# Two PSUM copies moved from VectorE to ScalarE, and the first x transposes moved to the last quantise round

## The chip, the cores and the metric

One Trainium2 chip, all 8 of its cores, one program for all with different data. A core has TensorE (PE, matrix products and transposes into PSUM), VectorE (DVE), ScalarE (ACT), GpSimd (POOL, which here only issues transfers) and SyncE (SP, which only issues transfers). The metric is the device time in microseconds of the slowest core. There is no traffic between cores.

## The reference, cut to what matters

```python
def layer(x):            # x: 2 x 8192 x 1024, float32
    q, k, v = x @ Wq.T + bq, x @ Wk.T + bk, x @ Wv.T + bv   # 16 heads of 64
    q = rope_headaxis(q) / 8;  k = rope_headaxis(k)          # angle by head index
    # sliding window: a query sees keys from 256 before it to 256 after it
    ctx = softmax(q k^T + window mask) v
    x = layernorm(x + ctx @ Wo.T + bo)
    xd, wd = mx_fp6(x), mx_fp6(W)      # blocks of 32 along a row, scale = max|.|/7.5,
    return layernorm(x + xd @ wd.T + bias)   # values rounded to an e2m3 grid
```

## The kernel before

Each core owns 2048 rows of x (16 tiles of 128) and gets two more tiles on each side, 20 in all. Products of float32 matrices are made as three bf16 products: every operand is split into a high part (an ACT activation that writes bf16, `*_hi`) and a low part (a DVE subtraction, `*_lo`). `split_evac` does this pair for a PSUM bank: ACT first, DVE behind it. All ordering between engines is worked out from a list of operations: each names the buffers it reads and writes, and each engine runs its own in the order of the list. An operation also waits for the earlier writer of its buffer on its own engine. `barrier()` makes the next operation of every engine wait for the last of all of them.

The program has four parts.

1. **Weights** (to 198 us). Wq, Wk and a piece of Wv are loaded, transposed, folded with the rope factors, and split.
2. **Quantise rounds** (198 to 351 us). The ffn weight has 8 row tiles, two per round `jp` = 0 to 3. A round is 28 steps, `qsteps`: two chains of 14 (one on the `qsc` tiles, one on `wfp`) laid alternately, so steps 0, 2, 4 ... are the one and 1, 3, 5 ... the other. Steps 8 and 9, 16 and 17, 22 and 23 run on ACT, all others on DVE. Between the steps, at the positions in `ins_at`, `vblocks` are put in: blocks of 4 transposes on PE into one PSUM bank and a `split_evac`. Rounds 0 to 2 have 4 `wv_block`s each (banks `pb[0]`, `pb[1]`); rounds 0 and 1 have two `x_pre_block`s more (banks `pb[2]`, `pb[3]`), which transpose the first two x tiles, `x_tm`, into `x_hi`, `x_lo`. With six blocks they sit behind steps 3, 7, 11, 15, 19, 23, with four behind 5, 11, 17, 23. Round 3 has none. After its steps each round transposes its two ffn tiles (4 blocks, banks `pb[2]`, `pb[3]`), splits them into three staging buffers `wfst`, and POOL writes them out with 8 transfers, each waiting for the one before. With three buffers the fourth split of a round waits for the first pair of transfers. The weight tiles of the rounds come through SP's queue (`wraw<-wf`); the two `x_tm` loads of round 0 stand in that queue behind the first three of them. A barrier ends this part.
3. **Attention** (351 to 1915 us). Ten passes `p` of two tiles. A pass makes k and v of its tiles on PE (`proj2`, evacuated by ACT), transposes v back in 4 blocks, alternately in banks `pb[0]` and `pb[1]`, and copies each bank into `v_tm` (line 877, DVE). Passes 2 to 9 then run 8 attention groups, numbered 0 to 7 here (two query tiles times four groups of 4 heads). After groups 1 and 3 come the load and transposes of the next x tiles, after group 5 the q projection (not in pass 9). A group (`att_group`) has 5 key tiles: PE makes scores, ACT the exponential into `probs`, DVE multiplies the first and the last with a triangle mask, PE multiplies with `v_tm` into `cbank`. At its end ACT takes the logarithm and the exponential of the row of sums (`zr`). The division follows one group later, in `tail`: PE spreads `zr` over 64 rows of `pb[3]`, DVE copies that to `zb_sb` and multiplies `cbank` with it into `ctxF`; `tail_split` then makes `cxh` and `cxl` on DVE. A tail is run after the last product of the next group and ahead of that group's `zr`. At most two pending pieces are run per group, so that behind a `spill` (after group 3) the pieces come in other pairs: groups 1 to 4 run tail and split together, group 5 spill and tail, groups 6 and 7 the split of the older group and then a tail. What is left is run at the start of the next pass (`flush_tail`).
4. **Output part** (from 1915 us): Wo, layernorms, quantised ffn. The change does not touch it.

Of the kernel before, what the change touches and what calls it, by code (L numbers as in the profile page):

```python
# [7 lines left out]
AF = mybir.ActivationFunctionType  # L8
# [176 lines left out]
def build_nc():  # L185
# [42 lines left out]
    pb = []  # L228
# [4 lines left out]
    pbuf = [Buf(f"pb{i}") for i in range(4)]  # L233
# [31 lines left out]
    def act(out_ap, in_ap, func, bias, scale, reads, writes, accum=None):  # L265
        P.op("act", lambda e, o=out_ap, i=in_ap, f=func, b=bias, s=scale,
             a=accum: e.activation(o, i, f, bias=b, scale=s, accum_out=a),  # L267
             reads=list(reads), writes=list(writes))
# [16 lines left out]
    def vcopy(eng, out_ap, in_ap, reads, writes):  # L285
        P.op(eng, lambda e, o=out_ap, i=in_ap: e.tensor_copy(o, i),  # L286
             reads=list(reads), writes=list(writes))
# [10 lines left out]
    def split_evac(psum_ap, psum_buf, hi_ap, lo_ap, wbufs):  # L298
        act(hi_ap, psum_ap, AF.Identity, 0.0, 1.0, [psum_buf], list(wbufs))
        tt("dve", lo_ap, psum_ap, hi_ap, ALU.subtract,  # L300
           [psum_buf] + list(wbufs), list(wbufs))
# [270 lines left out]
    x_tm_b = [Buf(f"x_tm{i}") for i in range(2)]  # L572
    x_fm_b = [Buf(f"x_fm{i}") for i in range(4)]

    def x_pre_block(j, half):
        fs = j
        bank = pb[2 + half]
        for k4 in range(4):
            kc = half * 4 + k4
            transp(x_tm[:, j * D + kc * 128: j * D + (kc + 1) * 128],  # L580
                   bank[:, k4 * 128:(k4 + 1) * 128], ident[:],
                   [x_tm_b[j], ident_b], [pbuf[2 + half]])
        split_evac(bank[:], pbuf[2 + half],
                   x_hi[:, fs * D + half * 512: fs * D + (half + 1) * 512],
                   x_lo[:, fs * D + half * 512: fs * D + (half + 1) * 512],
                   [x_fm_b[fs], wtmp_b[0], bias_tm_b["bq"]])
# [8 lines left out]
    for jp in range(4):  # L595
# [11 lines left out]
        vblocks = []  # L607
        if jp < 3:
            for vsl in range(2):
                vjt = 2 * jp + 2 + vsl  # L610
                for vhalf in range(2):
                    vblocks.append(
                        lambda vsl=vsl, vjt=vjt, vhalf=vhalf: wv_block(
                            wvraw[vsl][:], wvraw_b[vsl], vjt, vhalf, vhalf))
        if jp == 0:
            for j in range(2):
                dma_load("sp", x_tm[:, j * D:(j + 1) * D],
                         xp[j * 128:(j + 1) * 128, :],
                         [], [x_tm_b[j], (cosr_b, sinr_b)[j]])
        if jp < 2:  # L620
            for half in range(2):
                vblocks.append(
                    lambda j=jp, half=half: x_pre_block(j, half))
        ins_at = ((3, 7, 11, 15, 19, 23) if len(vblocks) > 4
                  else (5, 11, 17, 23))
        for i, f in enumerate(qsteps):
            f()
            if i in ins_at and ins_at.index(i) < len(vblocks):
                vblocks[ins_at.index(i)]()
        if jp < 2:  # L630
            for sl in range(2):
# [4 lines left out]
        for sl in range(2):  # L636
            jt = 2 * jp + sl
            st = jt % 3
            for half in range(2):
                bank = pb[2 + half]  # L640
                wi = (jt * 2 + half) % 3
                for k4 in range(4):
# [7 lines left out]
                                                    b=128),  # L650
                           wfst_lo[wi][:].rearrange("p (a b) -> p a b",
                                                    b=128),
                           [wfst_b[wi]])
                for scr, stg in ((wf_scr_hi, wfst_hi[wi]),
                                 (wf_scr_lo, wfst_lo[wi])):
                    dst = bass.AP(scr.tensor,
                                  scr.offset + (half * 4) * D + jt * 128,
                                  [[8 * D, 128], [D, 4], [1, 128]])
                    P.dma("gp", lambda e, d=dst, s=stg: e.dma_start(
                        out=d, in_=s[:].rearrange("p (a b) -> p a b",  # L660
                                                  b=128)),
# [16 lines left out]
    v_tm_b = [Buf(f"v_tm{i}") for i in range(VR)]  # L678
# [6 lines left out]
    zb_sb = sb("zb_sb", [64, 512], a_scope);  zb_sb_b = Buf("zb_sb")  # L685
# [48 lines left out]
    def att_group(tq, g):  # L734
# [18 lines left out]
        if True:  # L753
# [40 lines left out]
            def tail(g=g, cbank=cbank, cbank_b=cbank_b):  # L794
                mm(m4[0:1, 0:64], zr[:], pb[3][0:64, :], True, True,
                   [m4_b, zr_b], [pbuf[3]])
                vcopy("dve", zb_sb[:], pb[3][0:64, :], [pbuf[3]], [zb_sb_b])
                tt("dve", ctxF[:], cbank[0:64, :], zb_sb[:], ALU.mult,
                   [cbank_b, zb_sb_b], [ctxF_b])
            pending_tail.append(tail)  # L800

            def tail_split(g=g):
# [34 lines left out]
    for p in range(10):  # L837
        a = 2 * p
        j = a + 1
# [25 lines left out]
        for ti in range(2):  # L865
            vs = (a + ti) % VR
            for half in range(2):
                bank = pb[half]
                for c4 in range(4):
                    ch = half * 4 + c4  # L870
                    transp(q_fm[:, vscr_off + ti * D + ch * 128:
                                 vscr_off + ti * D + (ch + 1) * 128],
                           bank[:, c4 * 128:(c4 + 1) * 128], ident[:],
                           [vscr_bufs[ti], ident_b], [pbuf[half]])
                dst = strided(v_tm[:], vs * VW + half * 4 * 130,
                              [[130, 4], [65, 2], [1, 64]])
                vcopy("dve", dst,
                      bank[:].rearrange("p (a c b) -> p a c b", a=4, b=64),
                      [pbuf[half]], [v_tm_b[vs]])
        if 3 <= j <= 17:  # L880
            def projq(a=a, qsA=qsA, src_hi_fn=src_hi_fn,
                      src_lo_fn=src_lo_fn, src_bufs=src_bufs):
# [379 lines left out]
```

How the kernel before makes its waits and increments, by code:

```python
    def emit(self, eng_obj, eng_name, sems):  # L161
        for o in self.ops:
            if o.eng != eng_name:
                continue
            for k, v in o.waits:
                eng_obj.wait_ge(sems[k], v)
            if o.build is None:
                continue
            inst = o.build(eng_obj)
            if o.need_inc:
                inst.then_inc(sems[o.sem_key], 16 if o.is_dma else 1)
```

## Time and profile before

| | |
|---|---|
| median of the two runs | 2692.77 us (2626.21 and 2759.32) |
| the profiled execution | 2625.88 us; span of its slowest core 2624.3 us, of the eight 2611.6 to 2624.3 us |
| busy in the span | PE 1834.2 us (70%), DVE 800.1 (30%), ACT 670.1 (26%), POOL 58.2 (2%) |
| weights, 0 to 198 us | PE busy 41.5, DVE 89.2, ACT 40.2 |
| quantise rounds, 198 to 351 us | PE busy 28.9, DVE 93.7, ACT 44.0 |
| attention, 351 to 1915 us | PE busy 1322.7, DVE 292.8, ACT 416.6; mean granted PE clock 0.93 |
| output part, 1915 to 2624 us | PE busy 441.1, DVE 324.4, ACT 169.4; clock 0.78 |

How to read it: the busy shares are means over four parts with different limits. In the second part no engine is busy for much over half of the time, so what counts there is the order of dependent steps. In the third PE is busy for 85% of the time, and the question is what it waits for in the rest.

### The profile page before, as it was taken

Reading aid. Unit: us, or ns where it says so; the run is one execution under the profiler, and the core shown is the slowest. Engines: PE = TensorE matmul, PEld = TensorE weight load, DVE = VectorE, ACT = ScalarE, POOL = GpSimd, SP = SyncE. Lnnn points to the kernel's source line nnn. Section 1 sums busy time; section 2 is a strip of 40 time slices with the busy share of each in tenths; the row PEclk is TensorE's granted clock in tenths of the full one; section 3 lists DMA queues with packets and bytes.
Section 4 is the critical chain, followed back from the end, with each engine's and each line's share of the span. In section 5 each row is a group of like instructions: output and inputs, shape, how many; then the busy total and the mean of one; then the engine's idle time right before and its main releaser. Section 6 shows DMA issues by size and latency. Waiting matters only on the chain.

```text
span 2624.3 us, 36230 instructions; the slowest of 8 cores (2611.6 to 2624.3 us)
## 1 busy us (share of the span) xinstructions
PE 1834.2 (70%) x14760; PEld 1505.8 (57%) x14760; DVE 800.1 (30%) x1157; ACT 670.1 (26%) x1154; POOL 58.2 (2%) x92
## 2 busy tenths in 40 slices
PE   2212168978978878888789788788739767667444
PEld 2202157857757767667667567577528556556333
DVE  2467601021121121121221220211221455555443
ACT  1313311132232232222331322322312222222221
POOL 0001100000000000000000000000000000000000
PEclk9999999989989988999999989889859888888777
DMA  4103110000000000000000000000043011000000
GB/s 131 48 14 102 45 32 25 9 17 9 9 21 9 5 24 9 9 17 9 9 17 9 17 9 9 9 9 1 9 144 105 17 49 49 33 33 33 33 17 17
DMA packets 23711, 77.02 MB, mean 29 GB/s; under 512 B 3701, under 2 KB 4085, under 8 KB 23290
## 3 DMA queue, kind: packets, MB, share of 16 engines
q1 hardware_dynamic: 12250, 32.74, 4.1%
q0 software_dynamic: 7552, 25.17, 3.4%
q10 hardware_dynamic: 3744, 16.78, 2.1%
q8 instruction: 119, 1.95, 0.3%
q14 instruction: 46, 0.38, 0.0%
HBM read 53.71 MB, written 20.97 MB: 28 GB/s over the span
## 4 chain that ended last, share of the span: by engine, by line
PE 57%; DVE 21%; issue 9%; ACT 7%; DMA 5%; DVEq 1%; ACTq 0%; SPq 0%; POOL 0%; POOLq 0%
PE pb L257 42%; PE psE L258 5%; DVE probs L272 3%; PE pb L262 3%; PE psE L257 3%; ACT probs L267 3%; PE psO L258 2%; PE psO L257 2%; DVE x_hi L272 2%; ACT lnsc L267 1%; DVE qscW1b L272 1%; DVE ctxF L272 1%; DVE zb_sb L286 1%; DVE xdf_lo L272 1%; DVE xres L272 1%
## 5 line engine op out<-in xcount | busy, mean ns | idle before, releaser
L257 PE MATMUL pb<-probs,v_tm 128*65 128x128 f32 x2560 | 394.2, 303 | 193.3 <-DVE probs L272 193.3
L257 PEld LDWEIGHTS pb<-probs,v_tm 128*65 128x65 f32 x2560 | 312.3, 153 | 246.2 <-issue 229.7
L272 DVE TENSOR_TENSOR probs<-probs,m 128x512 f32<-128x512 f32 x128 | 88.2, 689 | 657.3 <-ACT probs L267 657.3
L267 ACT ACTIVATE probs<-psE,killb_sb 128x512 f32<-128x512 f32 x192 | 131.9, 687 | 288.9 <-PE psE L258 283.7
L257 PE MATMUL pb<-x_hi,wk_hi 128*128 128x256 bf16 x640 | 182.5, 285 | 24.8 <-DVE v_tm L693 23.1
L262 PE MATMUL pb<-ident,xdt 128*128 128x128 f32 x192 | 47.8, 409 | 200.3 <-DVE xdf_lo L272 103.4
L257 PE MATMUL pb<-x_lo,wk_hi 128*128 128x256 bf16 x640 | 182.6, 285 | 0.0
L257 PE MATMUL pb<-x_hi,wk_lo 128*128 128x256 bf16 x640 | 182.5, 285 | 0.0
L257 PE MATMUL pb<-x_hi,wv_lo 128*128 128x256 bf16 x640 | 174.4, 273 | 0.0
L257 PE MATMUL pb<-x_lo,wv_hi 128*128 128x256 bf16 x640 | 174.4, 273 | 0.0
L257 PE MATMUL pb<-x_hi,wv_hi 128*128 128x256 bf16 x640 | 174.4, 273 | 0.0
L286 DVE COPY v_tm<-pb 128x512 f32<-128x512 f32 x40 | 27.6, 691 | 463.0 <-PE pb L262 461.4
L258 PE MATMUL psE<-q_fm,k_fm 64*128 64x128 f32 x1536 | 157.7, 331 | 0.0
L262 PEld LDWEIGHTS pb<-ident,xdt 128*128 128x128 f32 x192 | 33.5, 210 | 213.9 <-issue 213.9
L258 PEld LDWEIGHTS psE<-q_fm,k_fm 64*128 64x128 f32 x1536 | 116.4, 213 | 55.1 <-issue 55.1
L257 PE MATMUL pb<-x_hi,wq_hi 128*128 128x256 bf16 x512 | 140.2, 274 | 0.0
L257 PE MATMUL pb<-x_hi,wq_lo 128*128 128x256 bf16 x512 | 140.1, 274 | 0.0
L257 PE MATMUL pb<-x_lo,wq_hi 128*128 128x256 bf16 x512 | 140.0, 273 | 0.0
L267 ACT ACTIVATE probs<-psO,killb_sb 128x512 f32<-128x512 f32 x128 | 87.7, 685 | 100.2 <-PE psO L258 100.2
L262 PE MATMUL pb<-ident,wraw 128*128 128x128 f32 x128 | 31.0, 423 | 105.9 <-DVE wraw L272 69.2
L267 ACT ACTIVATE k_fm<-pb,fm_bk 128x256 f32<-128x256 f32 x80 | 37.9, 474 | 230.6 <-PE pb L257 226.6
L272 DVE TENSOR_TENSOR xres<-pb,xres 128x512 f32<-128x512 f32 x32 | 22.1, 692 | 236.7 <-PE pb L262 232.9
(173 smaller groups left out, 3383.6 us busy)
## 6 DMA issues: line engine op xcount, KB each, us to landing
x_tm<-xp SPq DMA_DIRECT2D x20, 512.0 KB, 3.7
xres<-xp ACTq DMA_DIRECT2D x16, 512.0 KB, 3.7
out<-outs POOLq DMA_DIRECT2D x16, 512.0 KB, 3.1
wraw<-wq SPq DMA_DIRECT2D x8, 512.0 KB, 3.5
wraw<-wf SPq DMA_DIRECT2D x8, 512.0 KB, 4.6
ctx_scr_hi<-cxh POOLq DMA_DIRECT2D x16, 256.0 KB, 3.0
ctx_scr_lo<-cxl POOLq DMA_DIRECT2D x16, 256.0 KB, 3.0
xdt<-wo SPq DMA_DIRECT2D x8, 512.0 KB, 3.5
```

Of the source, the lines that this page charges most:

```text
L257: e.matmul(c, a, b, start=s1, stop=s2) if t is None else
L258: e.matmul(c, a, b, start=s1, stop=s2, tile_position=t),
L262: P.op("pe", lambda e, a=in_ap, o=out_ap, i=idn: e.transpose(o, a, i), reads=list(reads), writes=list(writes))
L267: a=accum: e.activation(o, i, f, bias=b, scale=s, accum_out=a),
L272: e.tensor_tensor(o, a, b, op=k),
L286: P.op(eng, lambda e, o=out_ap, i=in_ap: e.tensor_copy(o, i), reads=list(reads), writes=list(writes))
```

## The change

- `x_pre_block` uses banks `pb[0]` and `pb[1]` in place of `pb[2]` and `pb[3]`.
- The two `x_tm` loads and all four `x_pre_block`s move from rounds 0 and 1 to round 3. Each round now has four blocks, behind steps 5, 11, 17 and 23.
- The copy into `zb_sb` (64 of them, 64x512) is an ACT activation with Identity and no longer a DVE copy.
- The copy into `v_tm` (40 of them, 128x512, written in pieces of 64) likewise.

```diff
     def x_pre_block(j, half):
         fs = j
-        bank = pb[2 + half]
+        bank = pb[half]
...
-        if jp == 0:
+        else:
             for j in range(2):
                 dma_load("sp", x_tm[:, j * D:(j + 1) * D],
                          xp[j * 128:(j + 1) * 128, :],
                          [], [x_tm_b[j], (cosr_b, sinr_b)[j]])
-        if jp < 2:
-            for half in range(2):
-                vblocks.append(
-                    lambda j=jp, half=half: x_pre_block(j, half))
-        ins_at = ((3, 7, 11, 15, 19, 23) if len(vblocks) > 4
-                  else (5, 11, 17, 23))
+            for j in range(2):
+                for half in range(2):
+                    vblocks.append(
+                        lambda j=j, half=half: x_pre_block(j, half))
+        ins_at = (5, 11, 17, 23)
         for i, f in enumerate(qsteps):
             f()
-            if i in ins_at and ins_at.index(i) < len(vblocks):
+            if i in ins_at and vblocks:
                 vblocks[ins_at.index(i)]()
...
-                vcopy("dve", zb_sb[:], pb[3][0:64, :], [pbuf[3]], [zb_sb_b])
+                act(zb_sb[:], pb[3][0:64, :], AF.Identity, 0.0, 1.0,
+                    [pbuf[3]], [zb_sb_b])
                 tt("dve", ctxF[:], cbank[0:64, :], zb_sb[:], ALU.mult,
                    [cbank_b, zb_sb_b], [ctxF_b])
...
-                vcopy("dve", dst,
-                      bank[:].rearrange("p (a c b) -> p a c b", a=4, b=64),
-                      [pbuf[half]], [v_tm_b[vs]])
+                act(dst,
+                    bank[:].rearrange("p (a c b) -> p a c b", a=4, b=64),
+                    AF.Identity, 0.0, 1.0, [pbuf[half]], [v_tm_b[vs]])
```

The `else` belongs to `if jp < 3`, so its body runs in round 3 alone.

## Rows read from the trace of the kernel before

**Rows 1.** The page's chain that ended last, shares by engine.
```profile
PE 57%; DVE 21%; issue 9%; ACT 7%; DMA 5%; DVEq 1%; ACTq 0%; SPq 0%; POOL 0%; POOLq 0%
```
**Rows 2.** Timeline of DVE, rounds 1 to 3: start, us, engine, line, operation [idle before, releaser].
```profile
232.59 1.21 DVE L291 TENSOR_REDUCE qsW_bmw<-wraw 128x32 f32<-128x1024 f32 x1
...
255.46 1.22 DVE L272 TENSOR_TENSOR wraw<-wfp 128x1024 f32<-128x1024 f32 x1
...
266.68 1.21 DVE L291 TENSOR_REDUCE qsW_bmw<-wraw 128x32 f32<-128x1024 f32 x1
...
287.02 0.69 DVE L272 TENSOR_TENSOR wv_lo<-pb,wv_hi 128x512 bf16<-128x512 f32 x1 [1.90 <-ACT wv_hi L267]
...
291.04 1.22 DVE L272 TENSOR_TENSOR wraw<-wfp 128x1024 f32<-128x1024 f32 x1
...
303.86 1.21 DVE L291 TENSOR_REDUCE qsW_bmw<-wraw 128x32 f32<-128x1024 f32 x1
...
323.15 1.22 DVE L272 TENSOR_TENSOR wraw<-wfp 128x1024 f32<-128x1024 f32 x1
```
**Rows 3.** Timeline of DVE: first round's start, and the barrier.
```profile
199.29 1.22 DVE L291 TENSOR_REDUCE wfp<-wraw 128x32 f32<-128x1024 f32 x1 [1.77 <-DMA wraw<-wf]
...
350.64 0.14 DVE L693 MEMSET v_tm<- 128x96 f32 x1 [17.14 <-DMA wf_scr_lo<-wfst_lo]
```
**Rows 4.** Chain that ended last, in order of time: start, us, what.
```profile
191.45 7.75 DMA wraw<-wf
...
294.44 4.94 DMA wf_scr_hi<-wfst_hi
```
**Rows 5.** Timeline of all engines, from group 2's end to group 3's mask.
```profile
1116.31 0.59 ACT L267 ACTIVATE zr<-pb 1x512 f32<-1x512 f32 x1 [3.10 <-PE pb L257]
1116.32 0.68 DVE L286 COPY zb_sb<-pb 64x512 f32<-64x512 f32 x1 [2.31 <-PE pb L257]
...
1117.11 0.68 DVE L272 TENSOR_TENSOR ctxF<-pb,zb_sb 64x512 f32<-64x512 f32 x1
...
1117.65 0.69 ACT L267 ACTIVATE probs<-psE,killb_sb 128x512 f32<-128x512 f32 x1
...
1119.03 0.67 DVE L272 TENSOR_TENSOR probs<-probs,m 128x512 f32<-128x512 f32 x1
```
**Rows 6.** Timeline of all engines: start of group 7, then the flush behind it.
```profile
1194.24 0.69 ACT L267 ACTIVATE probs<-psE,killb_sb 128x512 f32<-128x512 f32 x1
1194.83 0.68 ACT L267 ACTIVATE probs<-psO,killb_sb 128x512 f32<-128x512 f32 x1
1195.03 0.69 DVE L272 TENSOR_TENSOR probs<-probs,m 128x512 f32<-128x512 f32 x1 [0.65 <-ACT probs L267]
...
1207.89 1.04 PE L257 MATMUL pb<-zr,m 1*64 1x512 f32 x2 [1.66 <-DVE ctxF L272]
```
**Rows 7.** Timeline of PE: third and fourth block of v transposes.
```profile
1074.46 0.63 PE L262 MATMUL pb<-ident,q_fm 128*128 128x128 f32 x4 [0.51 <-DVE v_tm L286]
...
1075.32 0.63 PE L262 MATMUL pb<-ident,q_fm 128*128 128x128 f32 x4 [0.24 <-DVE v_tm L286]
```
**Rows 8.** The page's costliest groups: busy us, mean ns | idle before, releaser.
```profile
L286 DVE COPY v_tm<-pb 128x512 f32<-128x512 f32 x40 | 27.6, 691 | 463.0 <-PE pb L262 461.4
```
**Rows 9.** ACT's instructions grouped by shape, same columns.
```profile
L267 ACT ACTIVATE wfp<-pb 128x512 f32<-128x512 f32 x32 | 19.1, 597 | 25.9 <-PE pb L262 24.1 <-DVE wq_lo L272 1.5
...
L267 ACT ACT_TABLE_LOAD x2 | 2.6, 1283 | 27.4 <-PE pb L262 27.4
```
**Rows 10.** Chain in order of time: zb_sb copies of groups 2, 3, 4, two passes.
```profile
932.19 0.69 DVE zb_sb L286
...
946.24 0.69 DVE zb_sb L286
...
962.45 0.69 DVE zb_sb L286
...
1297.07 0.69 DVE zb_sb L286
...
1311.10 0.69 DVE zb_sb L286
...
1325.79 0.69 DVE zb_sb L286
```

More of the change, by code:

```diff
@@ L581, in x_pre_block @@
                    bank[:, k4 * 128:(k4 + 1) * 128], ident[:],
-                   [x_tm_b[j], ident_b], [pbuf[2 + half]])
-        split_evac(bank[:], pbuf[2 + half],
+                   [x_tm_b[j], ident_b], [pbuf[half]])
+        split_evac(bank[:], pbuf[half],
                    x_hi[:, fs * D + half * 512: fs * D + (half + 1) * 512],
```

## The prediction

> **What bounds the kernel now.** I read the table by parts first, then the chain that ended last, then the timelines of each engine at the places that the edits touch. The chain is PE for 57% and DVE for 21%, with ACT at 7% [rows 1]. This says little alone: DVE is busy 30% of the span, so it is on the chain by its place in a sequence and not by its load. Taking work off DVE because it carries 21% of the chain would help only where the copy's result comes sooner or where something else on DVE was waiting behind it. So I go through the edits by place.
>
> **The x blocks, in the quantise rounds.** No transposes or splits are added or removed: four x blocks leave rounds 0 and 1 and four enter round 3. What counts is how long the 28 steps of a round take with 6, 4 and 0 blocks between them. From the first reduction to the end of the last product, the DVE timeline [rows 2] gives
>
> - round 1, six blocks: 255.46 + 1.22 - 232.59 = 24.09 us
> - round 2, four blocks: 291.04 + 1.22 - 266.68 = 25.58 us
> - round 3, none: 323.15 + 1.22 - 303.86 = 20.51 us.
>
> Four blocks take longer than six. The row of 287.02 shows why: the block behind step 23 has its ACT half queued behind two ACT steps of over 1 us, and DVE, in order, stands for 1.90 us until that half is done [rows 2]. With positions 5, 11, 17, 23 two of the four blocks (17 and 23) stand right behind such a pair of ACT steps; with 3, 7, 11, 15, 19, 23 only the last does. After the change all rounds have the four-block form. Round 1 gains 25.58 - 24.09 = 1.5 us in length, round 0 the same, round 3 25.58 - 20.51 = 5.1 us: 8.1 us more. A round's end is on the path throughout: the next begins behind its last split, and the last is followed by 8 written transfers in a line, at whose end the barrier stands (DVE is idle 17.14 us until the last of them) [rows 3]. These transfers hide nothing, because they start when the round's first split is done.
>
> Two transfers move as well. The `x_tm` loads stood behind three `wraw` loads in SP's queue; there the second `wraw` took 7.75 us [rows 4] and DVE waited 1.77 us for it [rows 3]. Without them at its side it should land sooner; the gain lies between 0 and 1.77 us, I take 1.5. In round 2 they now stand behind the last `wraw` load, and there POOL's first write already took 4.94 us beside that one load of 512 KB [rows 4]. The fourth split, and DVE behind it, waits for this write. With three loads beside it I take 1.5 us more, between 0 and 5 (twice as long). The x tiles themselves come several us before step 5 of round 3, and `pb[0]`, `pb[1]` are free by then, so the bank change costs nothing; if it did, it would be a wait for an older split, under 1 us. Sum of this edit: 8.1 - 1.5 + 1.5 = **+8 us**, between +4 and +13.
>
> **The zb_sb copy.** It is ready at 1116.32 and takes 0.68 on DVE; `ctxF` starts 0.79 later, and three DVE operations on, at 1119.03, the mask that PE waits for [rows 5]. On ACT a copy of 512 from PSUM with Identity takes 0.597 us, by the nearest group, for 128 rows and not 64 [rows 9], and DVE follows an ACT result at a distance of about 0.1 us (the mask at 1195.03 behind an activation ending at 1194.93) [rows 6]. So `ctxF` starts at 1116.31 + 0.60 + 0.10 = 1117.01 and no longer at 1117.11: the whole DVE row, mask included, comes 0.1 us sooner. But the copy stands on ACT ahead of `zr`'s two activations and the next `probs`. Overlapping neighbours start 0.59 us apart when one takes 0.69 [rows 6], so the copy holds ACT for 0.5 us. The first `probs` moves from 1117.65 [rows 5] to 1118.15, ends at 1118.84, and the mask could start at 1118.94; DVE is ready at 1118.93. In groups 1 to 4 the two are level: -0.1 us each.
>
> In groups 6 and 7 the split of the older tail is done early and only copy and product stand behind the tail. At the end of group 6 DVE sits idle 0.65 us until ACT's `probs` [rows 6]: here ACT is the later one already, and the copy delays it by 0.5 us. At the end of group 7 PE stands for 1.66 us ahead of the next tail's product [rows 6]; it needs `zr`'s second activation, and is delayed by 0.4 to 0.5. (The row names `ctxF` as releaser, but the code has no such dependence; both end within 0.2 us.) Behind group 5 stands the q projection, which covers it; group 0 has no tail. Per pass: -0.4 + 0.5 + 0.45 = +0.55 us, eight passes +4.4, and in the last pass, without a q projection behind group 5 and with the last tail ahead of the barrier, about 0.5 more: **+5 us**. Bounds: at best ACT's copy is hidden at groups 6 and 7 too (-0.1 x 48 = -5), at worst the 0.5 us counts at all 56 ends outside group 0 (+28).
>
> **The v_tm copy.** PE stood for 0.51 and 0.24 us ahead of the third and fourth block of transposes, each time until a DVE copy [rows 7] of 0.69 [rows 8]. At 0.60 on ACT each is 0.1 sooner: -0.2 us per pass, ten passes **-2 us**. The fourth copy now stands on ACT ahead of the first `probs`, but that one waits for PE's scores anyway. Writing in pieces of 64 is not shown for ACT; were it to take 0.2 us longer than on DVE, the edit would cost 0.4 x 10 = +4 us.
>
> What speaks against both ACT edits is the Trainium skill, "ScalarE: Activation LUTs", section on what ACT_TABLE_LOAD costs and the one on table sets: a switch to a function of another set costs a load of about 1.3 us and a drain, while the cheap functions such as identity are in every set. The trace has 2 loads of 1283 ns in the whole span [rows 9], though logarithm, exponential and Identity alternate in it hundreds of times; so far it agrees with the second half of the rule, and the sum holds no load.
>
> **Sum.** 2625.88 (the profiled execution) + 8 + 5 - 2 = 2637 us, 0.4% more. This execution agrees with the faster of the two runs (2626.21). The median shown, 2692.77, is the middle between that and 2759.32, and lies 67 us above it.
>
> **Rivals.**
>
> *The PE clock moves (faster).* The distance between the same two points in a pass, groups 3 and 4, is 962.45 - 946.24 = 16.21 us in one pass and 1325.79 - 1311.10 = 14.69 in another, with the same instructions; that from 2 to 3 is 14.05 and 14.03 [rows 10]. PE's clock is granted at one of two levels, and the stretches at the lower one come where they come. A shift of some tenths of a us can change which form a pass takes. If in every pass one more such interval were short, 8 x 1.5 = 12 us would go: 2625; if two, 2613. It decides over the sum above from eight intervals on. For it: both forms occur. Against it: nothing makes the shift go one way.
>
> *The same, the other way.* One or two more long intervals in each pass: 2649 or 2661. ACT's longer turn lengthens PE's stands, which makes this a bit likelier.
>
> *The x move is free.* If DVE's waits in round 3 took the blocks in, as four blocks of DVE work are only 4 x 0.6 us, the edit would cost nothing: 2629. Against it: round 2 against round 3.
>
> *Table loads (slower beyond doubt).* If Identity between `zr`'s logarithm and the `probs` exponential made ACT load tables, each of 64 tails would pay two loads of 1.283: 2637 + 164 = 2801. It decides from 20 such pairs on. Against it: the 2 loads of rows 9.
>
> *The moved loads collide* with POOL's writes by the full 5 us, and the round behind them starts late: 2641.
>
> **How the numbers follow.** Forecast 0.50, clock faster 0.14, clock slower 0.17, x move free 0.10, collision 0.06, table loads 0.03. The likeliest one's own range is 2625 to 2650 (the bounds of the terms, one at a time). The range reaches to the clock rivals, 2613 to 2661. Since the time to be held may be a median of few runs, like the 2692.77 here, with an execution of the long kind in it, 67 us above, I let the upper end reach to 2637 + 67 = 2704. A measurement of this kernel can tell about 2% from no change; 2% of 2626 is 52 us. All cases but the table loads stay inside it, with 0.03 more for terms off by much: faster 0.01, same 0.93, slower 0.06.
>
> **What the profile will show.** DVE's steps in rounds 0, 1 and 3 all take about 25.6 us, with two waits of 1.9 us in each; the memset behind the barrier stands about 8 us later. `zb_sb` on ACT takes about 0.6; groups 1 to 4 start their masks with DVE and ACT within 0.1 us of each other; in groups 6 and 7 `probs` is 0.5 later. ACT has 2 table loads. DVE's busy time falls by 64 x 0.68 + 27.6 = 71 us, ACT's rises by 104 x 0.6 = 62. I am wrong if round 3 stays near 20.5 us, if the interval from one pass to the next moves by over 2 us, or if ACT's copies take 0.8 us or more.

## The result, and the profile after

| | before | after |
|---|---|---|
| median | 2627.12 us | 2651.41 us |
| ratio, 95% interval | | 1.0095, 1.0084 to 1.0107 |
| profiled execution (span of its slowest core) | 2625.88 us (2624.3) | 2651.29 us (2649.8) |
| DVE, ACT busy on that core | 800.1, 670.1 us | 729.9, 730.5 us |

In some executions the cores of a die run slower whatever the kernel; such executions are left out of the ratios and such cores out of the means below, and 2692.77 was a median with one of them in it. The change makes the kernel 0.95% slower, 24 us; I had forecast 0.4%, 11 us. Here is the page of the profile after, its busy lines and the chain that ended last by engine, which answers to [rows 1]:

```profile
PE 1842.3 (70%) x14760; PEld 1507.6 (57%) x14760; DVE 729.9 (28%) x1053; ACT 730.5 (28%) x1258; POOL 58.2 (2%) x92
...
PE 56%; DVE 20%; issue 9%; ACT 9%; DMA 5%; DVEq 1%; ACTq 0%; SPq 0%; POOL 0%; POOLq 0%
```

DVE lost 70 us of work (71 forecast), ACT gained 60 (62 forecast), and the chain lost 1% of DVE and gained 2% of ACT. None of this tells of the 24 us. Three marks on the timelines do. In the mean of the eight cores the memset behind the barrier went from 347.5 to 354.5 us (+7.0), and the stretch from the first mask of pass 2 to the last mask of pass 9, which I call the attention part below, from 1376.1 to 1393.9 us (+17.8). Between these marks and behind them little changed (-1.6 and +2.2); the mean span went up by 25.3. So the first part came out near the forecast (+8), and the second, forecast at +3, did not.

**The quantise rounds.** DVE's timeline after, with the columns of [rows 2] and [rows 3]:

```profile
231.46 1.21 DVE L291 TENSOR_REDUCE qsW_bmw<-wraw 128x32 f32<-128x1024 f32 x1
...
255.41 1.22 DVE L272 TENSOR_TENSOR wraw<-wfp 128x1024 f32<-128x1024 f32 x1
...
304.55 0.69 DVE L272 TENSOR_TENSOR wfst_lo<-pb,wfst_hi 128x512 bf16<-128x512 f32 x1 [8.27 <-ACT wfst_hi L267]
305.16 1.21 DVE L291 TENSOR_REDUCE qsW_bmw<-wraw 128x32 f32<-128x1024 f32 x1
...
319.20 0.69 DVE L272 TENSOR_TENSOR x_lo<-pb,x_hi 128x512 bf16<-128x512 f32 x1 [1.90 <-ACT x_hi L267]
...
325.25 0.69 DVE L272 TENSOR_TENSOR x_lo<-pb,x_hi 128x512 bf16<-128x512 f32 x1 [1.90 <-ACT x_hi L267]
...
329.26 1.22 DVE L272 TENSOR_TENSOR wraw<-wfp 128x1024 f32<-128x1024 f32 x1
...
356.85 0.14 DVE L692 MEMSET v_tm<- 128x96 f32 x1 [17.26 <-DMA wf_scr_lo<-wfst_lo]
```

Round 3 takes 329.26 + 1.22 - 305.16 = 25.3 us, where it took 20.5, and shows the two waits of 1.90 at the blocks behind steps 17 and 23. Round 1 takes 255.41 + 1.22 - 231.46 = 25.2, where it took 24.1. The moved loads show in the chain in order of time, beside [rows 4]:

```profile
191.02 5.05 DMA wraw<-wf
...
294.02 6.66 DMA wf_scr_hi<-wfst_hi
```

The weight load took 2.7 us less without them, and the first write of round 2 took 1.7 us longer with them. Round 0 shows DVE's wait of 1.77 us for that load gone: on these two cores it got shorter by 1.0 us on the whole, from 26.3 to 25.3.

**A group's end with tail and split.** All engines after, the end of group 2, beside [rows 5]:

```profile
1125.80 0.59 ACT L267 ACTIVATE zb_sb<-pb 64x512 f32<-64x512 f32 x1 [3.10 <-PE pb L257]
1126.41 0.59 ACT L267 ACTIVATE zr<-pb 1x512 f32<-1x512 f32 x1
1126.56 0.68 DVE L272 TENSOR_TENSOR ctxF<-pb,zb_sb 64x512 f32<-64x512 f32 x1 [3.06 <-ACT zb_sb L267]
...
1127.75 0.69 ACT L267 ACTIVATE probs<-psE,killb_sb 128x512 f32<-128x512 f32 x1
...
1128.54 0.69 DVE L272 TENSOR_TENSOR probs<-probs,m 128x512 f32<-128x512 f32 x1
```

The copy takes 0.59 us, as forecast, but holds ACT for 0.61 (1126.41 - 1125.80), not 0.5: these neighbours do not overlap. And `ctxF` starts 0.76 behind its start, not 0.70. So ACT is the later one here too; the mask comes 2.74 us behind the copy's start, where it came 2.71. The forecast gain of 0.1 is a loss of 0.03.

**Group 6 and the flush**, beside [rows 6]:

```profile
1203.18 0.59 ACT L267 ACTIVATE zb_sb<-pb 64x512 f32<-64x512 f32 x1 [3.09 <-PE pb L257]
...
1205.92 0.69 DVE L272 TENSOR_TENSOR probs<-probs,m 128x512 f32<-128x512 f32 x1 [1.23 <-ACT probs L267]
...
1220.13 1.93 PE L257 MATMUL pb<-zr,m 1*64 1x512 f32 x2 [2.17 <-ACT zr L267]
```

DVE's idle time ahead of the mask went from 0.65 to 1.23, PE's ahead of the flush's product from 1.66 to 2.17, both close to the forecast 0.5. But the last row shows what the forecast had only as a rival: the same two matrix instructions take 1.93 us where they took 1.04 [rows 6]. The granted clock over them is 0.50 of full speed, where it was 1.00: they fell into a stretch at the lower of TensorE's two clock levels, 1.2 in place of 2.4 GHz.

**The passes.** With the time of the first mask of a pass as a mark, a pass can be read off two rows. Core 1 before, first masks of two passes running, and core 2 after:

```profile
1077.80 0.69 DVE L272 TENSOR_TENSOR probs<-probs,m 128x512 f32<-128x512 f32 x1 [1.05 <-ACT probs L267]
...
1258.54 0.69 DVE L272 TENSOR_TENSOR probs<-probs,m 128x512 f32<-128x512 f32 x1 [0.77 <-ACT probs L267]
```
```profile
1087.25 0.69 DVE L272 TENSOR_TENSOR probs<-probs,m 128x512 f32<-128x512 f32 x1 [46.67 <-ACT probs L267]
...
1271.61 0.69 DVE L272 TENSOR_TENSOR probs<-probs,m 128x512 f32<-128x512 f32 x1 [46.63 <-ACT probs L267]
```

180.7 us became 184.4. The seven passes from pass 2 on, by these marks:

| | lengths, us |
|---|---|
| before, core 1 | 181.8 181.2 184.1 180.7 180.9 181.3 183.9 |
| after, core 2 | 183.3 184.3 184.3 184.4 184.6 184.0 184.2 |

The kernel before mostly mixes two lengths, the changed one has only the longer. The waits that its copies add explain 0.7 us of a pass between groups (0.03 at four places, 0.61 at group 6) and 0.5 at the flush.

Busy time by window settles what the rest is. The columns are the window, its length, the busy time (and number of instructions) of PE, of its weight loads, of DVE, ACT and POOL, then the granted PE clock as a share of full speed. First the kernel before on core 1, a long pass, a short pass and the attention part; then the attention part of the changed kernel on core 2:

```profile
893.65:1077.80 184.15, 155.26 (x1264) 125.25 (x1264) 35.62 (x57) 49.83 (x85) 2.42 (x4) 0.92 0.05 13
1077.80:1258.54 180.74, 152.16 (x1264) 123.53 (x1264) 35.52 (x57) 49.81 (x85) 2.41 (x4) 0.93 0.05 13
530.64:1906.32 1375.68, 1152.32 (x9476) 931.09 (x9476) 272.45 (x430) 383.26 (x641) 18.14 (x30) 0.92 0.05 11
```
```profile
535.31:1929.09 1393.78, 1161.11 (x9476) 935.35 (x9476) 212.50 (x340) 436.07 (x731) 18.12 (x30) 0.91 0.05 11
```

PE runs 9476 matrix instructions in the attention part of either kernel and is busy with them for 8.8 us longer after the change. In the mean of the eight cores it is 8.5 us, the granted clock goes from 0.924 to 0.913, and PE's idle time goes up by 9.3 us, about as much as the waits above add in eight passes (8 x 1.2). So about half of the 17.8 us is longer waits and half is the clock.

### The profile page after: what moved, and what is told of

Its sections match the earlier page's. It is cut to its first block, busy times and chain, and to the rows that moved or that the text cites. A ratio compares the mean times of both kernels' runs of the same rounds, so it can differ in the third digit from the quotient of the medians.

```text
span 2649.8 us, 36265 instructions; the slowest of 8 cores (2633.7 to 2649.8 us)
## 1 busy us (share of the span) xinstructions
PE 1842.3 (70%) x14760; PEld 1507.6 (57%) x14760; DVE 729.9 (28%) x1053; ACT 730.5 (28%) x1258; POOL 58.2 (2%) x92
## 4 chain that ended last, share of the span: by engine, by line
PE 56%; DVE 20%; issue 9%; ACT 9%; DMA 5%; DVEq 1%; ACTq 0%; SPq 0%; POOL 0%; POOLq 0%
PE pb L257 42%; PE psE L258 4%; DVE probs L272 3%; PE pb L262 3%; PE psE L257 3%; ACT probs L267 3%; PE psO L257 2%; PE psO L258 2%; DVE x_hi L272 2%; ACT lnsc L267 1%; DVE qscW1b L272 1%; ACT zb_sb L267 1%; DVE ctxF L272 1%; DVE x_lo L272 1%; DVE xdf_lo L272 1%
## 5 line engine op out<-in xcount | busy, mean ns | idle before, releaser
L257 PEld LDWEIGHTS pb<-x_hi,wk_hi 128*128 128x128 bf16 x640 | 65.5, 102 | 46.5 <-issue 36.4
L272 DVE TENSOR_TENSOR ctxF<-pb,zb_sb 64x512 f32<-64x512 f32 x64 | 43.7, 683 | 173.9 <-ACT zb_sb L267 130.2
```

The lines of the kernel that those rows point to most:

```text
L257: e.matmul(c, a, b, start=s1, stop=s2) if t is None else
L272: e.tensor_tensor(o, a, b, op=k),
```

## The experiments

All edits are to the kernel before unless said otherwise. "Attention part" is the mean over the eight cores, or over as many as are said behind it, of the stretch defined above; "barrier" is the start of the memset behind it in the mean of all eight. The passes are the seven measured as above. A stand is the time from the start of a group's last mask to the start of the next group's first.

### One edit at a time: x_only, zb_only, v_only

```diff
# x_only: the change's edits to x_pre_block and to the rounds, both copies on DVE
# zb_only
-                vcopy("dve", zb_sb[:], pb[3][0:64, :], [pbuf[3]], [zb_sb_b])
+                act(zb_sb[:], pb[3][0:64, :], AF.Identity, 0.0, 1.0,
+                    [pbuf[3]], [zb_sb_b])
# v_only
-                vcopy("dve", dst,
+                act(dst,
...
-                      [pbuf[half]], [v_tm_b[vs]])
+                    AF.Identity, 0.0, 1.0, [pbuf[half]], [v_tm_b[vs]])
```

> Only the x blocks are moved; both copies stay on VectorE. Setup theory: the rounds take the four-block form (about 25.3 us each) and the moved loads hold up the fourth split of round 2, so the memset behind the barrier comes about 7 us later (346.3 to 353.1 us in the mean of the cores) and the time is 2627 + 7 = 2634 us, ratio 1.0027. The attention passes keep the two lengths that the kernel before has, 180.9 and 184.1 us. Rival (the whole difference of 24 us comes from the later start, because it shifts all that follows against the clock of TensorE): 2645 us or more, passes at 184 us.

> Only the zb_sb copy goes to ScalarE. Both theories expect the stand from a group's last mask to the next group's first to be 5.73 us at group 6 where it was 5.12, and about 0.5 us more ahead of the flush, some 1.1 us per pass. Theory of the two lengths: that pushes the passes from 180.9 to 184.2 us, by slow-clock stretches inside groups and at the flush, so 7 passes times (184.2 - 182.0 in the mean) = 15 us and about 1 in the last pass: 2643 us, ratio 1.006. Rival, sum of waits: 8 x 1.1 = 9 us: 2636 us, ratio 1.0034, passes at 182.0 and 185.2.

> Only the v_tm copy goes to ScalarE. The stretch from the first v transpose to the first probs falls from 3.84 to 3.61 us per pass. Sum of waits: -0.2 x 10 = -2 us, 2625. Theory of the two lengths: passes stay at 180.9 or 184.1 us, and the time is 2627 us plus or minus 5, by how many of them take the one or the other. Rival (ScalarE's strided writes are what costs): copies of over 0.8 us and 2635 us.

> v_only once more. If the long passes belong to this kernel and not to that execution, 5 to 7 of the seven passes are again at 184.3 us, the attention part is 1384 to 1392 us where it was 1376 before, and the time is 2635 to 2640 us. If it was chance, passes mix as before, 2625.

> zb_only once more, for a comparison: stands of 5.73 at group 6, all passes at 184.0 to 184.6 us on an undisturbed die, attention part 1393 to 1396 us, 17 to 20 more than before: 2645 us, ratio 1.007. That would put the copies' cost of the changed kernel on this edit, with nothing left for the v copies when both are made, although v_only costs 8 to 15 us alone. If the terms add, the changed kernel should have been at 2627 + 7 + 18 + 12 = 2664.

| | ratio (interval) | barrier | attention part | passes |
|---|---|---|---|---|
| before | | 347.5 | 1376.1 | mixed 180.9, 184 |
| after | 1.0095 (1.0084 to 1.0107) | 354.5 | 1393.9 | all 184 |
| x_only | 1.0054 (1.0006 to 1.0102) | 354.4 | 1374.7 | mostly 180.8, some 177.8, 183.9 |
| zb_only_b | 1.0101 (1.0058 to 1.0144) | 346.9 | 1395.4 (6 cores) | all 184 |
| v_only_b | none | 346.3 | 1385.7 | 184.3 after the first, 180.7 in some cores |

x_only confirms the first part: the barrier is 7 us later, as in the changed kernel, and the attention part is not longer for starting later. The ratio's interval is wide and holds the 1.0027 expected. It also shows how far the attention part moves with nothing changed inside it: 1369.6 to 1379.7 us by core, where the kernel before has 1374.5 to 1379.0.

zb_only_b, the same kernel as zb_only, has the whole longer attention part alone, +19 (zb_only gives 1394.9 over 4 cores). Its stand from the last mask of group 6 to the next group's first is 5.73 us on all cores where it was 5.12, and all its passes are long. It came out as the theory of the two lengths had it, somewhat above its 16, and above the sum of waits (+9).

v_only is the surprise. It came out at 1383.8 to 1392.8 us in the first profile and 1380.5 to 1391.8 in the second, +10 in the mean, although the stretch it touches got shorter, from 3.84 to 3.62 us between the first v transpose and the first `probs`. And the terms do not add: 7 + 19 + 10 would be 36 us, the changed kernel has 25. There is no ratio for this kernel. The profiled execution of v_only_b took 2631.3 us, under the 2635 to 2640 expected: its first passes up to the first mark take 2.2 us less than before, and the mean span of its cores is 5 us longer and not 10.

The v rows of the changed kernel, PE and ACT, beside [rows 7], and ACT's new groups by shape, beside [rows 8] and [rows 9]:

```profile
1267.93 2.81 ACT L267 ACTIVATE v_tm<-pb 128x512 f32<-128x512 f32 x4 [0.98 <-PE pb L262]
...
1268.67 1.37 PE L262 MATMUL pb<-ident,q_fm 128*128 128x128 f32 x8 [0.40 <-ACT v_tm L267]
```
```profile
L267 ACT ACTIVATE zb_sb<-pb 64x512 f32<-64x512 f32 x64 | 37.8, 590 | 191.0 <-PE pb L257 191.0
...
L267 ACT ACTIVATE v_tm<-pb 128x512 f32<-128x512 f32 x40 | 23.9, 597 | 14.0 <-PE pb L262 9.8
...
L267 ACT ACT_TABLE_LOAD x2 | 2.6, 1283 | 27.8 <-PE pb L262 27.8
```

PE waits 0.40 ahead of the third block (0.51 before) and 0.11 ahead of the fourth (0.24 before), which the row of eight transposes holds in its 1.37 us. Writing in pieces of 64 costs ACT nothing: 597 ns, the same as for whole rows. And 104 more Identity activations among logarithms and exponentials brought no table load.

### Where the zb_sb copy costs: zb_14, zb_57, zb_6

```diff
-                vcopy("dve", zb_sb[:], pb[3][0:64, :], [pbuf[3]], [zb_sb_b])
+                if zb_act:     # zb_14: tq % 2 == 0   zb_57: tq % 2 == 1
+                               # zb_6: tq % 2 == 1 and g == 1
+                    act(zb_sb[:], pb[3][0:64, :], AF.Identity, 0.0, 1.0,
+                        [pbuf[3]], [zb_sb_b])
+                else:
+                    vcopy("dve", zb_sb[:], pb[3][0:64, :], [pbuf[3]],
+                          [zb_sb_b])
```

> The zb_sb copy goes to ScalarE only for the tails of groups 0 to 3, which run at the ends of groups 1 to 4, where VectorE was the later one. If the cost sits at group 6 and the flush, where ScalarE was already the later one, these places cost nothing: 5.73 us where it was 5.71, 2627 us plus or minus 4, and the passes keep both lengths. If any activation ahead of zr costs its 0.6 us, 4 x 0.5 x 8 = 16 us: 2643 us.

> The other half of zb_14: the zb_sb copy goes to ScalarE only for the tails of groups 4 to 7, which run at the ends of groups 5, 6, 7 and in the flush. If the cost of this edit sits where ScalarE was already the later one, nearly all of zb_only's 17 to 20 us in the attention part is here: 1390 to 1396 us, passes at 184.0 to 184.6, where zb_14 had 1378 to 1385 us and mixed passes. If the cost comes from any shift of the pass, it is shared: 1380 to 1386 us.

> The copy goes to ScalarE for one tail per pass, that of group 5, run at the end of group 6. The stand there grows from 5.12 to 5.73 us. By itself 8 x 0.6 = 5 us: attention part 1381 us. Theory of the lengths in steps: the passes stay within 0.3 us of 177.8, 180.9 or 184.3, and the part is 1376 to 1396.

| | ratio (interval) | attention part | stand at group 6 | passes |
|---|---|---|---|---|
| zb_14 | 1.0021 (0.9991 to 1.0050) | 1381.7 | 5.12 | mixed |
| zb_57 | 1.0075 (1.0053 to 1.0097) | 1395.7 (6 cores) | 5.73 | all 184.3, the first up to 185.6 |
| zb_6 | 1.0050 (1.0030 to 1.0070) | 1387.8 | 5.73 | mixed, more of 184 |

The masks of zb_57 on core 0, last of group 6 and first of group 7, with the copy between:

```profile
1188.86 0.69 DVE L272 TENSOR_TENSOR probs<-probs,m 128x512 f32<-128x512 f32 x1 [6.10 <-ACT probs L267]
...
1191.85 0.59 ACT L267 ACTIVATE zb_sb<-pb 64x512 f32<-64x512 f32 x1 [3.09 <-PE pb L257]
...
1194.60 0.69 DVE L272 TENSOR_TENSOR probs<-probs,m 128x512 f32<-128x512 f32 x1 [1.23 <-ACT probs L267]
```

1194.60 - 1188.86 = 5.74. The same edit at the four places where DVE's row was the later one costs 6 us in the attention part, a little more than the 4 allowed for, and at the places where ACT was, 20. So the step of the prediction which told the places apart was right. Here too the terms do not add: zb_only_b, with all of these copies, has 19. And one copy per pass, 0.61 us at one place, costs 1387.8 - 1376.1 = 11.7 us and not 8 x 0.61 = 4.9.

### Added time without a moved copy: d16_g6, d256_g6

```diff
             act(zr[:], zr[:], AF.Exp, 0.0, -1.0, [zr_b], [zr_b])
+            if tq % 2 == 1 and g == 2:     # N = 16 or 256
+                act(dum[:, 0:N], cbank[0:64, 0:N], AF.Identity, 0.0, 1.0,
+                    [cbank_b], [dum_b])
```

> The kernel before with one more activation (64x16, result not used) behind zr at group 6 of each pass, nothing else. By the lengths of ScalarE's work it adds about 0.2 us at one place per pass. Sum of waits: 8 x 0.2 = 2 us, 2629. Theory of the lengths in steps: a pass stays within 0.3 us of 177.8, 180.9 or 184.3 us, so the added time is either swallowed or grows to 3.4 us in a pass; the attention part (1376 us from first to last mask before) moves by anything from -5 to +18 us.

> The same with 64x256, about 0.4 us at one place per pass. Sum of waits: 8 x 0.4 = 3 us, 2630, passes at about 181.3 and 184.5. Theory of the lengths in steps: passes again near 177.8, 180.9 or 184.3 us, more of them long than with the shorter one: 2630 to 2645.

The stand at group 6 grew by less than I had set out to add: to 5.18 us with 16 columns and 5.38 with 256. The attention part is 1376.5 us (6 cores) and 1380.3 us (4 cores). The ratio of d256_g6 is 1.0014 (0.9979 to 1.0049), no more than the sum of waits; d16_g6 has none. Together with zb_6:

| stand at group 6, added | attention part, added | 8 times the stand |
|---|---|---|
| 0.06 us (d16_g6) | 0.4 us | 0.5 us |
| 0.26 us (d256_g6) | 4.2 us | 2.1 us |
| 0.61 us (zb_6) | 11.7 us | 4.9 us |

At 0.61 us more than twice the added wait comes out. At 0.26 us it can't be told: the four cores have 1377.7 to 1381.4 us, and x_only spreads as far with nothing added. In these three kernels no pass behind the first took a length more than 0.6 us off 177.8, 180.9 or 184.3.

### Is it ScalarE or the timing: v_back, v_back2

```diff
# both: v_only, and behind the four copies of a pass
+        act(dum[:, 0:128], ident[0:64, 0:128], AF.Identity, 0.0, 1.0,   # v_back
+            [ident_b], [dum_b])
+        for _ in range(2):                                              # v_back2
+            act(dum[:, 0:40], ident[0:64, 0:40], AF.Identity, 0.0, 1.0,
+                [ident_b], [dum_b])
```

> v_only with one more activation (64x128, 0.29 us, result not used) behind the four copies, so that the first probs of a pass starts about 0.2 us later, near where it did with the copies on VectorE. Theory that the slow-clock stretches fall by when TensorE's work comes and the pass has a length in steps: passes go back to 180.9, some 184, the attention part to 1374 to 1380 us and the time to 2627, although work was added. Rival (the copies on ScalarE cost 3.4 us per pass by themselves): 1384 to 1392 us plus 8 x 0.2, 2640.

> v_back did not move what it was to move: its extra activation fell into a gap, and the first probs stood 3.63 us behind the first v transpose as in v_only (3.62), not 3.84. Here two activations of 64x40, the second waiting for the first, are to put it at 3.8. If the length of a pass hangs on the time between these points, passes go back to a mix with 180.9 and the attention part to 1374 to 1382 us, where v_only_b has 1385.7 in the mean of the cores. If something else of the move to ScalarE makes the passes long, it stays at 1384 to 1392 us.

In v_back the added activation fell into a gap and the first `probs` stood at 3.63 us behind the first v transpose, as in v_only; passes stayed at 184.3, the attention part was 1388.3 us (7 cores) and the ratio 1.0067 (1.0048 to 1.0087). So an added activation that moves nothing leaves the long passes. v_back2 puts that distance at 1060.77 - 1056.88 = 3.89 us (3.84 before, 3.62 in v_only). PE's v transposes, then ACT, core 0:

```profile
1056.88 1.06 PE L262 MATMUL pb<-ident,q_fm 128*128 128x128 f32 x8 [1.28 <-ACT q_fm L267]
```
```profile
1060.31 0.55 ACT L267 ACTIVATE dum<-ident 64x40 f32<-64x40 f32 x2
1060.77 0.67 ACT L267 ACTIVATE probs<-psE,killb_sb 128x512 f32<-128x512 f32 x1
```

First masks of two passes running, v_only_b on core 4 and v_back2 on core 2:

```profile
1072.60 0.69 DVE L272 TENSOR_TENSOR probs<-probs,m 128x512 f32<-128x512 f32 x1 [47.03 <-ACT probs L267]
...
1256.92 0.69 DVE L272 TENSOR_TENSOR probs<-probs,m 128x512 f32<-128x512 f32 x1 [47.04 <-ACT probs L267]
```
```profile
1073.29 0.69 DVE L272 TENSOR_TENSOR probs<-probs,m 128x512 f32<-128x512 f32 x1 [47.33 <-ACT probs L267]
...
1254.15 0.69 DVE L272 TENSOR_TENSOR probs<-probs,m 128x512 f32<-128x512 f32 x1 [47.37 <-ACT probs L267]
```

184.3 us against 180.9. The attention part is 1370.9 us in the mean of the eight cores (1368.0 to 1373.0), 15 us less than v_only_b with *more* work in it, less than the kernel before, and below the 1374 to 1382 expected. The two kernels hold the same copies on the same engine; they differ by the two small activations and 0.27 us of start time once per pass. The profiled execution took 2619.69 us; in the mean span of the cores it is 10 us less than v_only_b, since the stretch from the barrier to the first mark is longer by 2.5 and that behind the last mask by 2.1. So it is the timing and not the engine, as far as one execution on eight cores shows it.

Where do the 3.4 us of a long pass come from? From the inside of groups. From DVE's first to its last mask a group takes 6.8 us when all of it is at the full clock, mostly 8.3 with one stretch at the lower level, and up to 9.7 with two. This is group 3 in v_only_b, 1121.87 - 1112.23 = 9.64:

```profile
1112.23 0.68 DVE L272 TENSOR_TENSOR probs<-probs,m 128x512 f32<-128x512 f32 x1
1121.87 0.69 DVE L272 TENSOR_TENSOR probs<-probs,m 128x512 f32<-128x512 f32 x1 [8.96 <-ACT probs L267]
```

and this is group 3 in v_back2, 1122.82 - 1114.48 = 8.34, the same instructions:

```profile
1114.48 0.68 DVE L272 TENSOR_TENSOR probs<-probs,m 128x512 f32<-128x512 f32 x1
...
1122.82 0.69 DVE L272 TENSOR_TENSOR probs<-probs,m 128x512 f32<-128x512 f32 x1 [7.66 <-ACT probs L267]
```

Busy time by window of these two stretches and of the two passes, first v_only_b, then v_back2 (columns as above):

```profile
1112.23:1121.87 9.64, 8.82 (x56) 7.31 (x56) 0.68 (x3) 2.06 (x3) 0.00 (x0) 0.65 0.00 1
1072.60:1256.92 184.32, 155.94 (x1264) 125.79 (x1264) 32.85 (x53) 52.21 (x89) 2.42 (x4) 0.91 0.05 12
```
```profile
1114.48:1122.82 8.34, 7.52 (x56) 6.26 (x56) 0.68 (x3) 2.06 (x3) 0.00 (x0) 0.80 0.00 1
1073.29:1254.15 180.86, 152.26 (x1264) 122.72 (x1264) 32.85 (x52) 52.40 (x91) 2.41 (x4) 0.93 0.05 13
```

56 matrix instructions on either side, at a granted clock of 0.65 and 0.80, take 8.82 and 7.52 us of PE; DVE and ACT are busy for the same time. Over the pass it is 1264 instructions on both sides, 0.91 against 0.93, and 155.94 - 152.26 = 3.7 us of PE, which is the 3.5 us between the passes.

With the same split for the other kernels, PE's busy and idle time in the attention part move apart. Against the kernel before, in the mean of the cores:

| | PE busy | PE idle |
|---|---|---|
| after | +8.5 us | +9.3 us |
| zb_14 | +5.0 | +0.7 |
| zb_57 (6 cores) | +10.3 | +9.3 |
| zb_6 | +7.2 | +4.5 |
| v_only_b | +11.4 | -1.8 |
| v_back2 | -4.7 | -0.5 |

The idle column is what the sum of waits tells of. The busy column is what it leaves out.

### Taking the tail off the path: late, late_pos, late_pos_zbv

```diff
# late
             for kp in range(5):
...
+                if kp == 1 and pending_tail:
+                    pending_tail.pop(0)()          # ln_exp of the group before
                 if kp >= 1:
                     ctx_mms(kp - 1)
+                if kp == 2:
+                    flush_tail()                   # tail, tail_split, spill
             ctx_mms(4)
-            if pending_tail:
-                pending_tail.pop(0)()
-            if pending_tail:
-                pending_tail.pop(0)()
-            act(zr[:], cbank[64:65, :], AF.Ln, 0.0, 1.0,
-                [cbank_b], [zr_b])
-            act(zr[:], zr[:], AF.Exp, 0.0, -1.0, [zr_b], [zr_b])
+            def ln_exp(cbank=cbank, cbank_b=cbank_b):
+                act(zr[:], cbank[64:65, :], AF.Ln, 0.0, 1.0, [cbank_b], [zr_b])
+                act(zr[:], zr[:], AF.Exp, 0.0, -1.0, [zr_b], [zr_b])
+            pending_tail.append(ln_exp)
# late_pos: also
-        ins_at = ((3, 7, 11, 15, 19, 23) if len(vblocks) > 4
-                  else (5, 11, 17, 23))
+        ins_at = ((3, 7, 11, 13, 15, 21) if len(vblocks) > 4
+                  else (7, 11, 15, 21))
# late_pos_zbv: late_pos with both copies on ACT
```

> The kernel before, but with zr's two activations behind the second probs of the next group, and the whole tail behind its third: VectorE's four operations and ScalarE's two no longer stand between a group's last mask and the next group's first. If the order of the tail is what bounds the group ends, the stand from last mask to first mask falls from 5.71 to about 3.5 us at groups 2 and 4, from 5.12 to 3.5 at group 6, from 4.12 to 3.5 at group 0; inside a group about 1 us is added for the product and the activations moved there. Pass 181 to 184 becomes 170 to 178: 2627 - 30 to 90, so 2540 to 2600 us. If TensorE's work and its clock bound the passes, less than 10 us is gained: 2617 to 2627.

> The same with the blocks of the quantise rounds behind steps 7, 11, 15, 21 (four) and 3, 7, 11, 13, 15, 21 (six), so that no block stands right behind a pair of ScalarE steps. If the 1.9 us waits come from that place alone, they go, round 2 takes about 22 us where it took 25.6 and rounds 0 and 1 about 23.2 where they took 24.1: 5 us less than the kernel late. If VectorE's half of a block costs its time wherever it stands, no change against it.

> late_pos with both copies on ScalarE. With the tail behind the third probs of the next group no one waits for it, so the zb copy costs or gives nothing there: stands of 3.47 us at groups 0, 2, 4, 6 as in late_pos, at most 0.6 us more at the flush of each pass; 2505 us plus or minus 10, by the lengths of the passes. If ScalarE's load is what costs, the insides of groups grow by 0.5 us each, 32 us in all: 2537.

| | ratio (interval) | barrier | attention part | passes |
|---|---|---|---|---|
| late | 0.9591 (0.9539 to 0.9644) | 347.1 | 1255.6 (6 cores) | 164.8, 166.7, 170.6 |
| late_pos | 0.9542 (0.9503 to 0.9581) | 338.3 | 1262.4 | the same |
| late_pos_zbv | 0.9547 (0.9526 to 0.9567) | 338.8 | 1260.4 | the same |

The passes lie mostly near these three lengths. The attention part of late is 120 us shorter, and its passes lie below the 170 to 178 us that I had given. The stands account for less than half of that: PE's idle time fell by 51 us, and its busy time for the same work by 69, with the granted clock at 0.976 where it was 0.924. Of all engines in late_pos, the end of group 2 and the start of group 3:

```profile
1055.85 0.69 DVE L272 TENSOR_TENSOR probs<-probs,m 128x512 f32<-128x512 f32 x1 [0.34 <-ACT probs L267]
...
1058.52 0.69 ACT L267 ACTIVATE probs<-psE,killb_sb 128x512 f32<-128x512 f32 x1 [2.78 <-PE psE L258]
1059.11 0.68 ACT L267 ACTIVATE probs<-psO,killb_sb 128x512 f32<-128x512 f32 x1
1059.31 0.69 DVE L272 TENSOR_TENSOR probs<-probs,m 128x512 f32<-128x512 f32 x1 [2.77 <-ACT probs L267]
1059.81 0.59 ACT L267 ACTIVATE zr<-pb 1x512 f32<-1x512 f32 x1
```

1059.31 - 1055.85 = 3.46 us from mask to mask, where it was 5.71, and nobody stands in between but the scores and the exponential themselves. The logarithm comes behind both `probs`. The x transposes profit too (7.91 to 5.42 at groups 1 and 3). This is what moving one copy to another engine could not give: the copy was one of six operations in that row, and it was in the row on either engine. With the tail off the path, late_pos_zbv and late_pos do not differ: 0.9547 against 0.9542, within both intervals, and the 2505 us expected of late_pos_zbv came out (2506).

DVE in late_pos, round 2 from its first reduction to its last product, and the barrier:

```profile
261.12 1.21 DVE L291 TENSOR_REDUCE qsW_bmw<-wraw 128x32 f32<-128x1024 f32 x1
...
281.14 1.22 DVE L272 TENSOR_TENSOR wraw<-wfp 128x1024 f32<-128x1024 f32 x1
...
339.71 0.14 DVE L693 MEMSET v_tm<- 128x96 f32 x1 [16.85 <-DMA wf_scr_lo<-wfst_lo]
```

Round 2 takes 21.2 us, where it took 25.6, without a wait of 1.90. The barrier comes 8.8 us sooner than in late, more than the 5 expected; but the attention part is 6.8 us longer than late's, and the two ratios' intervals overlap. I did not run these positions with the old group ends.

## Why the prediction was right or wrong

**The x move: right, and near by its parts.** +8 forecast, +7.0 measured. Rounds of 25.2 to 25.3 us (25.6 forecast), two waits of 1.90 each, the first load sooner, the first write of round 2 longer by 1.7 (1.5 forecast). The rival that the move is free falls. late_pos shows that the positions are the cause of these waits, since the waits go with them.

**The v_tm copy: its own stretch right, its effect wrong.** The stretch got shorter by 0.22 us as forecast, the kernel longer. The step that failed is the silent one that a shorter stand on the path makes a shorter kernel: in v_only_b PE is idle for 1.8 us less and busy for 11.4 us more.

**The zb_sb copy: the places right, two sizes off.** The step "overlapping neighbours start 0.59 us apart when one takes 0.69, so the copy holds ACT for 0.5 us" took the overlap of two `probs`; the copy and the logarithm behind it overlap by nothing (0.61 us apart), so groups 1 to 4 lose 0.03 each instead of gaining 0.1, and group 6 loses 0.61. This is 0.6 us a pass more than I had. The range had a slip as well: by its own bound of +28 for this edit the likeliest case reached to 2660 and not to 2650. ACT's result also reached DVE's `ctxF` 0.17 us after the copy's end and not 0.10.

**The sum: wrong by the clock, and by the size of the waits.** Of the 17.8 us, 6.0 lie in the stands between groups of passes 2 to 8 (4.3 of them at group 6), 3.0 in the last pass, 5.3 inside groups and 3.5 in the stretches from group 7 to the next pass, which hold the longer wait at the flush. By engine it is 9.3 us of longer waits of PE, where the sum had 3, and 8.5 us in which TensorE's instructions are the same and only more of them fall at the lower clock level, where the sum had nothing. I had this as a rival, "the same, the other way", and gave it 0.17 with a price of 12 us for one more long interval per pass; the changed kernel has it, at about two thirds of the price. My reason for not making it the likeliest was that "nothing makes the shift go one way". That is the step that failed: with the copies in place every core of the changed kernel, whatever its start, had only long passes. My own sign of being wrong, an interval from pass to pass that moves by over 2 us, came true (180.7 to 184.4).

In the kernels with the old group ends nearly all passes behind the first lie within 0.6 us of 177.8, 180.9 or 184.3, on eight cores with different starts. The kernel before stood mostly at 180.9: of its seven passes 2.3 in the mean of the cores are over 182.5. With waits added it is 2.8 in d256_g6, 3.3 in zb_14, 4.9 in zb_6, and all seven in zb_57 and in the changed kernel. What I could have read from the trace of before is that its seven passes take mostly two lengths; I looked at intervals between groups [rows 10] and took their scatter for chance.

What stays open is why the passes have these lengths, and which length a given edit will choose: v_only (shorter by 0.2 us) takes the longer, v_back2 (longer by 0.05) the shorter with some of 177.8, and x_only, with nothing changed inside a pass, has some of 177.8 too. I can't derive that from the waits. That each pass contains as much as it does of the low level because of the stands inside it is argued; late, whose stands are shorter, has a granted clock of 0.976 in place of 0.924, which speaks for it, and also three lengths.

**Table loads.** The rival of 0.03 falls: 2 loads, as before [rows 9]. The Trainium skill, "ScalarE: Activation LUTs", section on table sets, has identity in every set, and the trace agrees, with 104 more Identity activations and no load more.

## What to carry to other kernels

A share of an engine on the chain says that its operations are in a row that others wait for, not that the engine is short of time; moving one operation of the row to another engine leaves the row as long (0.9591 came from moving the row, 1.0101 from moving the copy). Before a block is put between steps of another engine, look at what stands ahead of its first half in that engine's queue: a place of two steps sooner was worth about 1.9 us each time. Where repeated passes of a kernel have only a few lengths, changes below a us per pass can't be summed from waits; measure them, split the difference into busy and idle time of the engine that bounds them, and prefer edits that are worth several steps. Shorter stands paid twice here: in late more than half of the gain was the same matrix work done at a higher mean clock.

## What the runs showed of the hardware

- The same 1264 matrix instructions of a pass, in one kernel on one core, with DVE and ACT busy for the same time within 0.1 us, take 180.74 or 184.15 us: PE is busy for 152.16 or 155.26 us. In v_back2 against v_only_b 0.27 us of a later start per pass gave back 15 us of the attention part in all, in one execution each.
- An activation on ACT starts 0.59 us behind one of 0.69 when neither waits (two `probs`), but 0.61 behind one of 0.59 (the copy, then the logarithm). Why the second pair does not overlap I did not separate.
- Behind two activations of 64x40, which take 0.55 us together, the next starts 0.46 us after the start of the first; behind one of 64x128 it starts 0.20 us after.
